# Residual loads moved ahead of the prefetch: two 512 KB loads of x issued one block earlier on ScalarE's queue

## The chip, the cores and the metric

The kernel runs as one program on the 8 cores of one Trainium2 chip. Each core computes one of the 8 batch entries, with no traffic between cores. The metric is device time in microseconds (us) of the slowest core.

## The reference, cut to what matters

```python
xn = _layernorm(x)                      # x: (8, 2048, 1024) f32, one batch entry per core
x = x + attn(xn) + ffn(xn)

def attn(x):                            # a linear recurrence over T=2048, written as a scan
    xn2 = layernorm(x) * ln_gamma + ln_beta
    y = scan(h = dA*h + dB*xn2;  y = C.h + D*xn2)
    return x + y @ W_out.T + b_out

def ffn(x):
    h = gelu(x @ ternary(W1).T + b1)    # 1024 -> 4096
    return h @ ternary(W2).T + b2       # 4096 -> 1024
```

The last step of the kernel computes, for each of 16 tiles of 128 rows, `h @ W2.T + y @ W_out.T` on TensorE and adds x (scaled and shifted by the row statistics of the first layernorm, which gives x + xn) and the biases on VectorE.

## The kernel before, in words

The program is a row of blocks. At the end of each block all engines meet in a barrier (the `UNCONDITIONAL_BRANCH` rows in the order of instructions). Every engine has its own list of instructions, written out by hand, with waits on semaphores between engines. DMAs are issued by SyncE (SP), by ScalarE (ACT) and by GpSimd (POOL) through the helper `sdma` (line 226), so every DMA issue shows line 226 in the profile. An instruction that ScalarE issues, be it a DMA or an activation, waits for all that stand ahead of it in ScalarE's list.

The stages: the statistics and normalization of x; a moment form of the recurrence, while the absolute sums of W1 and W2 are taken (activation L694, matmul L782); the first product of the feed-forward part (L1027), whose result goes through Gelu (L946) to tile `hst` and by SP to the scratch tensor `scr_h` in memory, while the ternary W2 is transposed into `W2T`. Then come the two blocks that the change touches.

The **W_out block** (lines 1084 to 1146). When `scr_h` is written, SP and ACT prefetch the hidden activations of the first two token groups (tg 0 and 1, 256 rows each) into the two buffers `hgrp`: SP loads the 16 even chunks of each group, ACT the 16 odd ones, so each issues 32 DMAs of 64 KB (128 rows of 512 bytes). POOL loads `bias1bc`, a row of 4 KB repeated to 128 partitions. Behind its 32 issues, in the same list, ACT converts the eight 128x1024 blocks of W_out to bf16 (`wob`, L1117); TensorE transposes each block (L1127) and VectorE copies it to `WoT` (L44 through a helper). The first two blocks of W_out are loaded earlier; POOL loads the other six into `wch`, each when ACT has converted the block two before it.

```python
for eb in range(8):
    swt(ac, f"w1c{eb % 2}", 16 * (eb // 2 + 1))
    if eb >= 2:
        ac.wait_ge(s_te, E_te_wo(eb - 2))
    bump(ac.activation(wob[eb % 2][:, :], wchunk[eb % 2][:, :], ...), "a2")
```

The **output block** (lines 1148 to 1237), 8 groups of 2 tiles (`tk` 0 and 1). TensorE makes 2 x (32 + 8) matmuls for a tile (L1186 with `hgrp` and `W2T`, L1193 with `yT` and `WoT`) into `ps_c` or `ps_e`. VectorE waits for the tile of x (`xr0` or `xr1`, 512 KB, 128 rows of 4 KB) and for TensorE, and makes four operations (line 44), and POOL stores the result. ACT only issues DMAs here. For the group tg it waits until TensorE is done with group tg-2 and issues 16 loads of `hgrp` (from tg 2 on), and then the two loads of `xr`, each (from tg 1 on) when VectorE is done with the tile of group tg-1 in the same buffer.

Of the kernel before, what the change touches and what calls it, by code (L numbers as in the profile page):

```python
# [98 lines left out]
def build_nc(debug_taps=False, stop_after=None):  # L99
    nc = bass.Bass("TRN2", target_bir_lowering=False)  # L100

    def din(name, shape, dtype=F32):
        return nc.dram_tensor(name, shape, dtype, kind="ExternalInput")

    x_in = din("x", [T, D])
# [40 lines left out]
    with st:  # L146
# [63 lines left out]
        def bump(inst, which, n=1):  # L210
            inst.then_inc(SEM[which], n)
            ctr[which] += n
            return ctr[which]
# [10 lines left out]
        def sdma(q, name, out, in_):  # L224
            s = streams[name]
            q.dma_start(out, in_).then_inc(s["sem"], 16)  # L226
            s["n"] += 16
            return s["n"]

        def swt(eng, name, val=None):  # L230
            s = streams[name]
            eng.wait_ge(s["sem"], s["n"] if val is None else val)  # L232
# [40 lines left out]
        with nc.Block() as blk:  # L273
            @blk.vector
            def _(dv):
                dv = _DR(dv)
                bump(dv.memset(xsq[:, :], 0.0), "dv")
# [793 lines left out]
        xr = [enD(nc.sbuf_tensor(f"xr{i}", [128, D], F32)) for i in range(2)]  # L1071
# [11 lines left out]
        with nc.Block() as blk:  # L1083
            @blk.gpsimd
            def _(gp):
                swt(gp, "srw", 16)
                swt(gp, "hw0", b5_hwv[0])
                swt(gp, "hw1", b5_hwv[1])
                sdma(gp, "cst", bias1bc[:, :], bass.AP(scr_rows, 0, [[0, 128], [1, D]]))
                for eb in range(2, 8):  # L1090
                    gp.wait_ge(s_a2, E_a2_wo(eb - 2))
                    sdma(gp, f"w1c{eb % 2}", wchunk[eb % 2][:, :],
                         Wout.ap()[eb * 128:(eb + 1) * 128, :])
            b6_cst = streams["cst"]["n"]

            @blk.sync
            def _(sy):
                swt(sy, "hw0", b5_hwv[0])
                swt(sy, "hw1", b5_hwv[1])
                for tg in range(2):  # L1100
                    for fc in range(0, 32, 2):
                        sdma(sy, f"hge{tg % 2}", hgrp[tg % 2][:, fc * 256:(fc + 1) * 256],
                             scr_h.ap()[fc, :, tg * 256:(tg + 1) * 256])

            @blk.scalar
            def _(ac):
                swt(ac, "hw0", b5_hwv[0])
                swt(ac, "hw1", b5_hwv[1])
                for tg in range(2):
                    for fc in range(1, 32, 2):  # L1110
                        sdma(ac, f"hgo{tg % 2}", hgrp[tg % 2][:, fc * 256:(fc + 1) * 256],
                             scr_h.ap()[fc, :, tg * 256:(tg + 1) * 256])
# [4 lines that stand above are left out]
                    bump(ac.activation(wob[eb % 2][:, :], wchunk[eb % 2][:, :],  # L1117
                                       AF.Copy, bias=0.0, scale=2.0), "a2")

            @blk.tensor  # L1120
            def _(te):
                for eb in range(8):
                    te.wait_ge(s_a2, E_a2_wo(eb))
                    if eb >= 1:
                        te.wait_ge(s_dv, E_dv_wo(eb - 1))
                    for dblk in range(8):
                        inst = te.transpose(ps_d[:, dblk * 128:(dblk + 1) * 128],  # L1127
                                            wob[eb % 2][:, dblk * 128:(dblk + 1) * 128],
                                            cID[:, :])
                    bump(inst, "te")  # L1130

            @blk.vector
            def _(dv):
                dv = _DR(dv)
                swt(dv, "hw0", b5_hwv[0])
                swt(dv, "hw1", b5_hwv[1])
                for eb in range(8):
                    dv.wait_ge(s_te, E_te_wo(eb))
                    bump(dv.tensor_copy(WoT3[:, :, eb * 128:(eb + 1) * 128], ps_d3), "dv")
# [8 lines left out]
        with nc.Block() as blk:  # L1148
# [8 lines left out]
            @blk.scalar  # L1157
            def _(ac):
                ac = _DR(ac)
                for tg in range(8):  # L1160
                    if tg >= 2:
                        ac.wait_ge(s_te, E_te_o(tg - 2, 1))
                        for fc in range(1, 32, 2):
                            sdma(ac, f"hgo{tg % 2}",
                                 hgrp[tg % 2][:, fc * 256:(fc + 1) * 256],
                                 scr_h.ap()[fc, :, tg * 256:(tg + 1) * 256])
                    for tk in range(2):
                        tci = tg * 2 + tk
                        if tg >= 1:
                            ac.wait_ge(s_dv, E_dv_oe(tg - 1, tk))  # L1170
                        sdma(ac, f"xr{tk}", xr[tk][:, :],
                             x_in.ap()[tci * 128:(tci + 1) * 128, :])

            @blk.tensor
            def _(te):
# [101 lines left out]
```

## Time and profile before

| what | us |
|---|---|
| two timed runs | 1138.73 and 1244.46, median 1191.6 |
| the profiled execution, its own time | 1137.69 |
| its span on the slowest core (core 7) | 1136.1 |
| spans of the eight cores | 1127.2 to 1136.1 |

The profile is that of core 7 in one execution. The span runs from the first to the last instruction on the core; 1.6 us of the execution's own time lie around it. In the picture of 40 slices each slice is 28.4 us long, a digit is the busy share in tenths. Times in the timeline are counted from the start of the span. "ACTq" and "SPq" are the queues' own instructions, here the issues of DMAs by ScalarE and SyncE.

### The profile page before, as it was taken

How to read it: one execution, taken by the hardware profiler on the slowest of the kernel's cores; microseconds unless marked ns; L12 is line 12 of the kernel's file. 1: busy time of each engine (PE TensorE's matmuls, PEld its weight loads, DVE VectorE, ACT ScalarE, POOL GpSimd, SP SyncE). 2: the span in 40 equal slices, each digit the busy share in tenths (PEclk: the TensorE clock that was granted, in tenths of full speed). 3: DMA queues.
4: the chain of work that ended last, by engine and by line, in shares of the span. 5: the costliest groups of instructions: out<-in, count | busy, mean ns of one | idle time of the engine just before them, and what ended most of it. 6: DMA issues, size and time to landing. Idle time of an engine off the chain costs nothing. (4 is left out here: it accounts for less than half of the span.)

```text
span 1136.1 us, 11816 instructions; the slowest of 8 cores (1127.2 to 1136.1 us)
## 1 busy us (share of the span) xinstructions
PE 755.1 (66%) x3622; PEld 321.7 (28%) x3622; DVE 430.1 (38%) x825; ACT 390.3 (34%) x481; POOL 109.2 (10%) x212
## 2 busy tenths in 40 slices
PE   0002222200899899819888888889049999999996
PEld 0000000100122122204444444444024444444442
DVE  3458888684354443422323232322011212212212
ACT  0033333200434344327888888887120000000000
POOL 1200000132111111100111111110010000000000
PEclk9999999999999999959999999999559999999998
DMA  4021111015555555523455545454641544345420
GB/s 72 1 70 55 57 57 53 14 25 98 174 173 166 154 178 178 176 62 142 168 179 184 175 171 181 168 179 155 169 164 38 135 126 127 80 127 148 113 73 38
DMA packets 78381, 136.41 MB, mean 120 GB/s; under 512 B 11448, under 2 KB 44656, under 8 KB 78320
## 3 DMA queue, kind: packets, MB, share of 16 engines
q0 software_dynamic: 22016, 67.64, 19.1%
q1 hardware_dynamic: 35568, 51.23, 14.5%
q10 hardware_dynamic: 20736, 16.79, 5.6%
q8 instruction: 31, 0.51, 0.2%
q14 instruction: 30, 0.25, 0.1%
HBM read 112.49 MB, written 25.19 MB: 121 GB/s over the span
## 5 line engine op out<-in xcount | busy, mean ns | idle before, releaser
L694 ACT ACTIVATE wabs<-wch 128x512 f32<-128x512 f32 x128 | 79.3, 628 | 122.7 <-DMA wch<-L_ffn_W 60.1
L1186 PE MATMUL ps_c<-W2T,hgrp 128*128 128x512 bf16 x512 | 115.7, 385 | 1.4 <-PEq L1083 1.4
L540 PE MATMUL ps_d<-sb_cID,xnb 128*128 128x128 bf16 x128 | 16.2, 306 | 149.5 <-ACT xnT L453 86.1
L1186 PE MATMUL ps_e<-W2T,hgrp 128*128 128x512 bf16 x512 | 113.1, 379 | 0.0
L795 PE MATMUL ps_c<-ub,sb_cP 128*128 128x512 bf16 x64 | 20.4, 450 | 82.4 <-DVE ub L717 82.4
L1186 PEld LDWEIGHTS ps_c<-W2T,hgrp 128*128 128x128 bf16 x512 | 50.7, 99 | 63.8 <-issue 5.0
L226 POOL DMA_DIRECT2D wch<-L_ffn_W x96 | 51.3, 535 | 175.8 <-ACT wabs L694 170.2
L1186 PEld LDWEIGHTS ps_e<-W2T,hgrp 128*128 128x128 bf16 x512 | 50.1, 98 | 60.4
L1027 PE MATMUL ps_a<-xnT,w1st 128*128 128x512 bf16 x256 | 62.2, 387 | 0.0
L712 DVE TENSOR_TENSOR ub<-xn2sb,mtb 128x512 bf16<-128x512 bf16 x128 | 45.7, 419 | 41.5 <-PE ps_c L799 23.2
L1027 PE MATMUL ps_b<-xnT,w1st 128*128 128x512 bf16 x256 | 60.6, 380 | 0.0
L1027 PE MATMUL ps_c<-xnT,w1st 128*128 128x512 bf16 x256 | 60.5, 379 | 0.0
L1027 PE MATMUL ps_e<-xnT,w1st 128*128 128x512 bf16 x256 | 60.5, 379 | 0.0
L782 PE MATMUL ps_a<-wabs,onesc 128*1 128x512 f32 x128 | 59.7, 610 | 0.0
L540 PEld LDWEIGHTS ps_d<-sb_cID,xnb 128*128 128x128 bf16 x128 | 12.4, 138 | 162.9 <-issue 162.9
L782 PE MATMUL ps_b<-wabs,onesc 128*1 128x512 f32 x128 | 58.0, 596 | 0.0
L990 DVE TENSOR_TENSOR w2tn<-wsgA,wsgB 128x1024 bf16<-128x1024 bf16 x32 | 22.1, 692 | 74.0 <-ACT wsgB L954 74.0
L44 DVE TENSOR_SCALAR t1f<-xr,stat_a,stat_b 128x1024 f32<-128x1024 f32 x8 | 6.5, 812 | 114.7 <-PE ps_c L1193 114.7
L984 DVE COPY w1st<-ps_d 128x1024 bf16<-128x1024 bf16 x30 | 20.7, 691 | 70.4 <-PE ps_d L1038 70.4
L44 DVE TENSOR_SCALAR t2f<-xr,stat_a,stat_b 128x1024 f32<-128x1024 f32 x8 | 6.5, 812 | 107.6 <-PE ps_e L1193 107.6
L934 ACT ACTIVATE wsgA<-wch,cst,invs 128x1024 bf16<-128x1024 f32 x30 | 37.2, 1240 | 29.0 <-DVE w2tn L990 27.9
L980 DVE TENSOR_TENSOR w1tn<-wsgA,wsgB 128x1024 bf16<-128x1024 bf16 x30 | 20.8, 693 | 61.0 <-ACT wsgB L937 61.0
(149 smaller groups left out, 1067.7 us busy)
## 6 DMA issues: line engine op xcount, KB each, us to landing
wch<-L_ffn_W SPq DMA_DIRECT2D x64, 256.0 KB, 3.5
wch<-L_ffn_W POOLq DMA_DIRECT2D x64, 256.0 KB, 3.9
wch<-L_ffn_W POOLq DMA_DIRECT2D x32, 512.0 KB, 5.4
wchC<-L_ffn_W POOLq DMA_DIRECT2D x32, 512.0 KB, 4.6
scr_h<-hst SPq DMA_DIRECT2D x32, 512.0 KB, 2.9
xt<-x SPq DMA_DIRECT2D x16, 512.0 KB, 3.3
hgrp<-scr_h SPq DMA_DIRECT2D x128, 64.0 KB, 4.1
hgrp<-scr_h ACTq DMA_DIRECT2D x128, 64.0 KB, 4.2
```

What stands on the lines that cost most here:

```text
L226: q.dma_start(out, in_).then_inc(s["sem"], 16)
L540: inst = te.transpose(ps_d[:, dblk * 128:(dblk + 1) * 128], xn_b[p][:, dblk * 128:(dblk + 1) * 128], cID[:, :])
L694: ac.activation(wabs[j % 4][:, :], wchunk[wk % 2][:, h * 512:(h + 1) * 512], AF.Abs).then_inc(s_wa, 1)
L712: dv._e.tensor_mul(u_b[k][:, hs], xn2sb[:, c * 1024 + h * 512: c * 1024 + (h + 1) * 512], mtb[:, k * D + h * 512: k * D + (h + 1) * 512])
L782: te.matmul(tgt[0:1, 0:512], onesc[:, 0:1], wabs[j % 4][:, :], start=(j % 16 == 0), stop=(j % 16 == 15)).then_inc(s_wm, 1)
L795: te.matmul(psy[:, sl], cP[:, k * 128:(k + 1) * 128], u_b[k][:, sl], start=(k == 0), stop=False)
L934: bump(ac.activation(wsgA[:, :], wchunk[k % 2][:, :], AF.Sign, bias=csl(C_NHALF), scale=invs[:, 0:1]), "a2")
L980: bump(dv.tensor_add(w1tn[:, :], wsgA[:, :], wsgB[:, :]), "dv")
L984: bump(dv.tensor_copy(w1st[k % 3].ap().rearrange("p (b f) -> p b f", f=128), ps_d3), "dv")
L990: bump(dv.tensor_add(w2tn[fc % 2][:, :], wsgA[:, :], wsgB[:, :]), "dv")
L1027: inst = te.matmul(psh, w1st[fc % 3][:, dblk * 128:(dblk + 1) * 128], xnT[:, dblk * T + t4 * 512: dblk * T + (t4 + 1) * 512], start=(dblk ...
L1186: te.matmul(pso[:, sl], hgrp[tg % 2][:, fc * 256 + tk * 128: fc * 256 + (tk + 1) * 128], W2T[:, fc * 1024 + dh * 512: fc * 1024 + (dh + 1) ...
```

## The change

The loads of `xr` for group 0 (both tiles) leave the output block, where they were ScalarE's first two instructions, and go to the W_out block, where they stand ahead of ScalarE's 32 loads of `hgrp`. In the output block the loads for the groups from 1 on stay where they were, with the same waits. Nothing else changes; the tiles `xr` are allocated before both blocks, and the semaphores count the same.

```diff
@@ -1106,6 +1106,9 @@
                 swt(ac, "hw0", b5_hwv[0])
                 swt(ac, "hw1", b5_hwv[1])
+                for tk in range(2):
+                    sdma(ac, f"xr{tk}", xr[tk][:, :],
+                         x_in.ap()[tk * 128:(tk + 1) * 128, :])
                 for tg in range(2):
                     for fc in range(1, 32, 2):
                         sdma(ac, f"hgo{tg % 2}", hgrp[tg % 2][:, fc * 256:(fc + 1) * 256],
@@ -1164,12 +1167,12 @@
-                    for tk in range(2):
-                        tci = tg * 2 + tk
-                        if tg >= 1:
+                    if tg >= 1:
+                        for tk in range(2):
+                            tci = tg * 2 + tk
                             ac.wait_ge(s_dv, E_dv_oe(tg - 1, tk))
-                        sdma(ac, f"xr{tk}", xr[tk][:, :],
-                             x_in.ap()[tci * 128:(tci + 1) * 128, :])
+                            sdma(ac, f"xr{tk}", xr[tk][:, :],
+                                 x_in.ap()[tci * 128:(tci + 1) * 128, :])
```

ScalarE's list in the W_out block and at the start of the output block, before and after (the line numbers of the kernel after are 3 higher from the first added line on):

```order
-L226 DMA hgrp<-scr_h 128x256 [waits st_hw0,st_hw1]
-L226 DMA hgrp<-scr_h 128x256 x31
-L1117 ACTIVATE wob<-wch 128x1024 [waits st_w1c0]
-L1117 ACTIVATE wob<-wch 128x1024 [waits st_w1c1]
...
+L226 DMA xr<-x 128x1024 [waits st_hw0,st_hw1]
+L226 DMA xr<-x 128x1024
+L226 DMA hgrp<-scr_h 128x256 x32
+L1120 ACTIVATE wob<-wch 128x1024 [waits st_w1c0]
+L1120 ACTIVATE wob<-wch 128x1024 [waits st_w1c1]
```

Two loads now stand between the barrier and the first load of `hgrp`, and every activation of the block stands behind 34 issues, where it stood behind 32. The second piece is again ScalarE's list, at the barrier between the W_out block and the output block:

```order
-L1157 UNCONDITIONAL_BRANCH [waits barrier_Pool_Activation_PE_DVE_SP_release]
-L226 DMA xr<-x 128x1024 x2
+L1160 UNCONDITIONAL_BRANCH [waits barrier_Pool_Activation_PE_DVE_SP_release]
 L226 DMA xr<-x 128x1024 [waits s_dv] x2
 L226 DMA hgrp<-scr_h 128x256 [waits s_te]
```

In the output block two loads without a wait are gone; the next rows are the same. The lists of the other four engines have the same instructions in the same places.

## Rows read from the trace of the kernel before

**Rows 1.** The page: the span in 40 slices of 28.4 us (busy tenths)
```profile
PE   0002222200899899819888888889049999999996
ACT  0033333200434344327888888887120000000000
DMA  4021111015555555523455545454641544345420
```

**Rows 2.** Timeline of core 7, the W_out block: start us, us, engine, line, what
```profile
801.56 20.45 SPq L226 DMA_DIRECT2D hgrp<-scr_h  x32
801.58 20.75 ACTq L226 DMA_DIRECT2D hgrp<-scr_h  x32
...
822.42 1.28 ACT L1117 ACT_TABLE_LOAD   x1 [24.65 <-issue]
823.71 2.00 ACT L1117 ACTIVATE wob<-wch 128x1024 bf16<-128x1024 f32 x2
...
825.33 0.53 POOL L226 DMA_DIRECT2D wch<-L_attn_W_out  x1 [22.72 <-ACT wob L1117]
...
829.79 1.06 ACT L1117 ACTIVATE wob<-wch 128x1024 bf16<-128x1024 f32 x1 [4.07 <-DMA wch<-L_attn_W_out]
...
845.58 0.69 DVE L44 COPY WoT<-ps_d 128x1024 bf16<-128x1024 bf16 x1 [1.98 <-PE ps_d L1127]
846.62 0.85 ACTq L226 DMA_DIRECT2D xr<-x  x2
...
846.91 9.63 PE L1186 MATMUL ps_c<-W2T,hgrp 128*128 128x512 bf16 x32 [1.44 <-PEq L1083]
...
858.11 7.07 PE L1186 MATMUL ps_c<-W2T,hgrp 128*128 128x512 bf16 x32
...
867.02 0.81 DVE L44 TENSOR_SCALAR t1f<-xr,stat_a,stat_b 128x1024 f32<-128x1024 f32 x1 [20.75 <-PE ps_c L1193]
```

**Rows 3.** Stretches of the output block: us, busy us (count) by engine, clock, DMA, GB/s
```profile
866.00:900.00 34.00, 34.00 (x160) 15.36 (x158) 7.08 (x8) 0.00 (x0) 1.07 (x2) 1.00 0.44 124
...
1060.00:1100.00 40.00, 40.00 (x187) 18.14 (x186) 7.83 (x9) 0.00 (x0) 1.59 (x3) 1.00 0.44 127
```

**Rows 4.** Instructions on tile xr: count, duration min/median/max ns; DMA to landing
```profile
L226 ACTq DMA_DIRECT2D xr<-x x16: 334/339/452, 846.6 to 1095.4; - x16
...
DMA to landing us min/median/max: 3.3/4.2/6.4
```

**Rows 5.** ScalarE's issues on tile hgrp: count, duration min/median/max ns
```profile
L226 ACTq DMA_DIRECT2D hgrp<-scr_h x128: 359/452/2659, 801.6 to 1070.8; - x128
```

**Rows 6.** Stretches of the prefetch: columns as in rows 3, the last three clock, DMA, GB/s
```profile
804.00:824.00 20.00, 0.00 (x0) 0.00 (x0) 0.00 (x0) 1.57 (x2) 0.00 (x0) 0.50 0.89 215
...
812.00:814.00 2.00, 0.00 (x0) 0.00 (x0) 0.00 (x0) 0.00 (x0) 0.00 (x0) 0.50 0.47 108
...
816.00:818.00 2.00, 0.00 (x0) 0.00 (x0) 0.00 (x0) 0.00 (x0) 0.00 (x0) 0.50 1.06 251
```

**Rows 7.** Stretches of the output block's first us, columns the same
```profile
848.00:849.00 1.00, 1.00 (x4) 0.30 (x2) 0.00 (x0) 0.00 (x0) 0.00 (x0) 0.50 0.91 352
849.00:850.00 1.00, 1.00 (x4) 0.45 (x3) 0.00 (x0) 0.00 (x0) 0.00 (x0) 0.50 1.03 406
...
852.00:853.00 1.00, 1.00 (x6) 0.50 (x5) 0.00 (x0) 0.00 (x0) 0.00 (x0) 0.93 0.00 0
```

**Rows 8.** DMA queues from 846 to 852 us: packets, MB, share of 16 engines
```profile
q10 hardware_dynamic: 287, 1.05, 46.5%
```

**Rows 9.** DMA queues from 801.5 to 810 us; q0 POOL's, q1 SP's, q10 ScalarE's
```profile
q0 software_dynamic: 144, 0.52, 25.9%
q1 hardware_dynamic: 708, 0.32, 17.0%
q10 hardware_dynamic: 637, 0.29, 12.6%
```

**Rows 10.** Timeline of core 0: its issues of the same block
```profile
795.88 17.63 ACTq L226 DMA_DIRECT2D hgrp<-scr_h  x32
```

## The prediction

> **What bounds the kernel now.** I read the picture of 40 slices first. TensorE is nearly full in the last 10 slices, and in the two before them it shows 0 and 4, while ScalarE shows 1 and 2 and the DMA engines 4 and 6 [rows 1]. That gap is the W_out block, the place where the change puts its two loads. Next the stretches of the output block: from 866 us on TensorE is busy 34.00 of 34.00 us and 40.00 of 40.00 us at the full granted clock [rows 3]. So once the output block runs, TensorE alone sets its end. ScalarE has only DMA issues there, and whatever delays the block's first matmul delays the end by as much.
>
> The timeline of the W_out block then shows what sets that first matmul [rows 2]. The barrier opens at about 801.5 us. ScalarE issues its 32 loads of `hgrp` for 20.75 us, up to 822.33. Only then come the table load (822.42) and the first two conversions of W_out (823.71). POOL's loads of further blocks of W_out wait for these (825.33, released by ScalarE's `wob`), ScalarE's third conversion waits for that load (829.79), and so on: load, convert, transpose, copy, until VectorE's last copy at 845.58. The barrier opens, and TensorE starts at 846.91. The two first conversions wait for nothing else: the idle time of 24.65 us ahead of the table load is given to "issue", and their data were there. So the path to the end is: 32 issues by ScalarE (20.75 us), the chain over W_out (822.33 to 846.91, 24.6 us), the output block. SyncE ends its issues at 822.01 as well, but no conversion waits for it.
>
> The 32 issues are not short because ScalarE is slow. One issue of `hgrp` takes 0.359 us at the least, 0.452 us in the median and 2.659 us at the most [rows 5]. At the median 32 would take 14.5 us; 20.75 us is 6.3 us more. During that stretch the DMA engines are busy 89% and move 215 GB/s, with single stretches at 1.06 and 251 GB/s [rows 6]. I read the long issues as ScalarE being held until its earlier transfers have moved. The Trainium skill ("DMA: Bandwidth & Descriptors", section "Issuing engines are not separate DMA queues") says that issuing from several engines saves only the sequencer's time and that this is usually small against the DMA itself; here the trace differs in what matters, since the issuing engine has work behind its issues and the 20.75 us of issuing are on the path.
>
> **The change, part by part.**
>
> *Removed: two issues at the start of the output block.* They take 0.85 us of ScalarE at 846.62 [rows 2], beside TensorE's matmuls, and nothing of ScalarE's is waited for there. Their data come 3.3 to 6.4 us after the issue [rows 4], so by 853.5 us at the latest. VectorE first reads them at 867.02, and there it is released by TensorE's `ps_c`, not by the load [rows 2]. The load had 13.5 us to spare. The gain is 0. Could it be more? The first 32 matmuls take 9.63 us where the next 32 take 7.07 [rows 2], and the loads of x move in just that time, so 2.56 us could be claimed for them. But until 852 the granted clock is 0.50 (1.2 GHz), and it was 0.50 all through the prefetch, in which TensorE had nothing to do [rows 6, 7]. The matmuls are slow by the clock, and nothing in the change makes TensorE busier before. I keep 0, with -2.56 us as the far bound.
>
> *Added: two issues ahead of the 32.* As bare instructions they cost 2 x 0.339 = 0.68 us on ScalarE [rows 4], and these are on the path, since every conversion stands behind them. This part no cover hides.
>
> *Added: 1.05 MB in a queue that is already held up.* By themselves the two loads took 46.5% of the 6 us from 846 to 852, that is 2.8 us of all 16 DMA engines [rows 8], at up to 406 GB/s [rows 7]. The prefetch has little free DMA time: 89% of 20 us leaves 2.2 us, much of it in single stretches such as that at 0.47 [rows 6]. From both sides: if the free time and the first 2.5 us, in which hardly anything moves, take in the loads, this costs 0; if they move at the mean rate of the prefetch, it is 1.05 MB / 215 GB/s = 4.9 us. I take 2.8 us, the engine time of the very same loads, as the nearest row. Here the loads of x would delay each later load of `hgrp` on ScalarE's queue, and by that its issue.
>
> *What stands behind.* The chain over W_out keeps its length. Its own loads start when the prefetch drains, before as after. The prefetched groups are not late: TensorE asks for group 0 only after the chain of 24.6 us. A later start of the output block moves all of it without changing it. ScalarE's further loads of `xr` wait for VectorE and TensorE as before. The allocation is the same and there is no new wait.
>
> The sum: 0 + 0.68 + 2.8 = +3.5 us. The profiled execution took 1137.69 us (its span 1136.1 and 1.6 us around it), so the forecast is 1137.7 + 3.5 = 1141.2 us. Of the two timed runs 1138.73 lies by this execution; the median of 1191.6 lies between it and 1244.46, which I do not use as a base.
>
> **The rivals.**
>
> *Hidden transfer (+0.7 us, 1138.4).* ScalarE's issues go on for 2.5 us before much data moves, and the DMA engines have 2.2 us free. If the loads of x fill these, only the two issues count. For it: core 0 issued its 32 in 17.63 us [rows 10], so not every core is held up as long as core 7. Against it: core 7 is the slowest core, and there 6.3 us of the issue time are already stalls.
>
> *SyncE gets ahead (+5.9 us, 1143.6).* Before, both queues run side by side and end together. While `bias1bc` with its 4 KB rows moved, it got 0.52 MB where the queues of `hgrp` got 0.32 and 0.29 [rows 9], 1.7 times one of them. If the loads of x share like this, SyncE's queue moves 1.05 / 1.7 = 0.62 MB meanwhile and is that far ahead, and ScalarE ends behind these bytes too: 0.62 MB / 251 GB/s = 2.4 us on top of the sum. For it: the queues share the same 16 engines. Against it: a queue that runs alone at the end is held up less, which gives part back. By the Trainium skill (same page, section "Queues, rings and completion order") each DMA engine takes turns between the queues packet by packet, which speaks for this rival; the rows show a share of 1.7 to 1 between large and small rows.
>
> *The slower side: a burst in which the memory collapses (+9.7 us or more, from 1147.4).* All eight cores now ask for their x at the same moment as for `scr_h`. If the loads moved at the rate of the poorest stretch, 108 GB/s [rows 6], they would cost 1.05 MB / 108 GB/s = 9.7 us. It becomes a slowdown by over 2% (22.8 us) only if the rate falls to 46 GB/s, or if ScalarE meets nine more stalls of the longest kind, 2.66 us [rows 5]. For it: issue times that differ between cores (17.63 and 20.75 us) and the poor stretch. Against it: 251 GB/s just after it, and 406 GB/s for these same loads when alone.
>
> *Faster after all (-5.4 us, 1132.3).* If large transfers at the head of ScalarE's queue made SyncE's queue wait and the rest of ScalarE's issues ran at their median, 34 issues would take 34 x 0.452 = 15.4 us, 5.4 us under 20.75. For it: core 0's 17.63 us lie on that side. Against it: there is more to move, and nothing takes work off. The 2.56 us of the slow matmuls, argued away above, would end on this side too.
>
> **How the numbers follow.** The forecast (stalls grow by about the loads' own DMA time) has a chance of 0.5, the hidden transfer 0.2, SyncE ahead 0.2, the collapse 0.06, the faster case 0.04. The first three lie between 1138.4 and 1143.6. Around each I put the difference that two executions show, as 1137.69 and 1138.73 here, and more where the slowest core may be another one (the cores' spans differ by 9 us). Down to the faster case's 1132.3 and up past the collapse's 1147.4 this gives a range of 1132.5 to 1151 us. A change by 2% is about what a measurement of this kernel can tell from none; that is 22.8 us either way, far outside of all sums. Faster by over 2%: 0.02, no case reaches it, only a disturbed comparison. Slower by over 2%: 0.04, the far end of the collapse. Within 2%: 0.94.
>
> **What would show it.** In the profile after: ScalarE's 34 issues from 801.5 us on should take about 24.3 us (20.75 + 3.5), by the hidden case 21.4, by SyncE's lead 26.6; SyncE should then end its 32 some 2 us or more before ScalarE. The table load to the first output matmul should again be 24.5 us, the 32 first matmuls again 9.6 us with the clock at 0.50, and VectorE's first operation on x again released by TensorE 20 us after the block's start. The reading is wrong if the issues take no longer than 20.75 us, if the time between table load and first matmul changes by over 2 us (then the loads of x disturb the loads of W_out), or if the first matmuls become faster. The prediction falls if the end moves by much more or less than the table load does.

## The result, and the profile after

| | us |
|---|---|
| before, median of 14 runs | 1136.76 |
| after, median of 15 runs | 1141.08 |
| ratio after to before | 1.0043, interval 1.0031 to 1.0056 |
| profiled execution after: its time, span of the slowest core (core 5) | 1144.99, 1143.5 |
| profiled execution before: the same (core 7) | 1137.69, 1136.1 |

The kernel became slower by 0.43%, that is 4.9 us (3.5 to 6.4) of 1136.76; the two medians of the table differ by 4.3 us, since the ratio is one of means. Runs in which one die of the chip ran at a lower clock are left out of the ratio; the 1244.46 us among the two times of before shown earlier was one of these.

The timeline of the slowest core after, in the W_out block. The rows answer to [rows 2]; the columns are the same.

```profile
805.03 22.49 SPq L226 DMA_DIRECT2D hgrp<-scr_h  x32
805.05 0.86 ACTq L226 DMA_DIRECT2D xr<-x  x2
805.56 0.53 POOL L226 DMA_DIRECT2D bias1bc<-scr_rows  x1 [18.53 <-POOLq L898]
805.94 23.02 ACTq L226 DMA_DIRECT2D hgrp<-scr_h  x32
829.04 1.28 ACT L1120 ACT_TABLE_LOAD   x1 [27.81 <-issue]
830.34 2.00 ACT L1120 ACTIVATE wob<-wch 128x1024 bf16<-128x1024 f32 x2
...
831.96 0.53 POOL L226 DMA_DIRECT2D wch<-L_attn_W_out  x1 [25.87 <-ACT wob L1120]
...
853.75 0.69 DVE L44 COPY WoT<-ps_d 128x1024 bf16<-128x1024 bf16 x1 [1.38 <-PE ps_d L1130]
...
855.08 8.87 PE L1189 MATMUL ps_c<-W2T,hgrp 128*128 128x512 bf16 x32 [1.44 <-PEq L1083]
...
874.42 0.81 DVE L44 TENSOR_SCALAR t1f<-xr,stat_a,stat_b 128x1024 f32<-128x1024 f32 x1 [19.98 <-PE ps_c L1196]
```

ScalarE issues from 805.05 to 828.96: 23.9 us, where it was 20.75 in [rows 2]. From the table load to the first output matmul it is 26.0 us (24.5 before on core 7), and VectorE's first operation on x is released by TensorE as before, so the early load gives nothing back. The block, from SyncE's first issue to the first output matmul, takes 50.05 us on this core and took 45.35 on core 7: 4.7 of the 7.4 us between the two spans. Another 3.5 us is where the block starts, 805.03 against 801.56, in stages that the change does not touch, and the output block is 0.8 us shorter. So the difference between these two single profiles (7.4 us) overstates the change; the ratio comes from many runs (4.9 us).

Since single cores scatter, the table below gives the mean over the eight cores of each profile, each number a difference between the starts of rows like those above: issue time is from SyncE's first issue to ScalarE's table load, chain from there to the first output matmul, rest from there to the end of the span.

| us, mean of 8 cores | issue time | chain | block | rest |
|---|---|---|---|---|
| before | 19.1 | 24.2 | 43.2 | 288.7 |
| after | 22.3 | 24.7 | 46.9 | 288.3 |
| difference | +3.2 | +0.5 | +3.7 | -0.4 |

What the change adds lies in the block, and there mostly in ScalarE's issues (3.2 of 3.7 us). The spans themselves grew by 5.6 us in the mean; the other 2.3 us are a later start of the block (798.8 us before, 801.1 after), in stages that the change does not touch. The block's length ranges from 41.6 to 45.4 us over the cores before, and from 43.9 to 50.1 after.

Where do the bytes go? The DMA queues of core 5 after, in the first 8 us of the block (packets, MB, share of the 16 engines; q10 is ScalarE's, q1 SyncE's, q0 POOL's), and the DMA share and rate in the stretch of the prefetch, which answers to [rows 6]:

```profile
q10 hardware_dynamic: 342, 1.08, 40.7%
q0 software_dynamic: 83, 0.34, 22.4%
q1 hardware_dynamic: 359, 0.17, 10.3%
```

```profile
805.00:824.00 19.00, 0.00 (x0) 0.00 (x0) 0.00 (x0) 0.00 (x0) 0.53 (x1) 0.50 0.87 207
824.00:829.00 5.00, 0.00 (x0) 0.00 (x0) 0.00 (x0) 0.00 (x0) 0.00 (x0) 0.50 1.01 251
```

In the first 8 us ScalarE's queue moves almost nothing but the loads of x, and SyncE's loads of `hgrp` get 0.17 MB through, where they got 0.32 MB in the first 8.5 us before [rows 9]. The engines are busy 87% up to 824 us and 101% from there to the end of the issues (a share of 1.01 means full), so the bytes that are still to move find no free room.

### The profile page after: what moved, and what is told of

It reads as the page before. It is cut to its first block and busy times, and to the rows that moved or that the text cites. A ratio compares the mean times of both kernels' runs of the same rounds, so it can differ in the third digit from the quotient of the medians.

```text
span 1143.5 us, 11816 instructions; the slowest of 8 cores (1129.9 to 1143.5 us)
## 1 busy us (share of the span) xinstructions
PE 756.9 (66%) x3622; PEld 321.3 (28%) x3622; DVE 430.3 (38%) x825; ACT 390.4 (34%) x481; POOL 109.2 (10%) x212
## 5 line engine op out<-in xcount | busy, mean ns | idle before, releaser
L795 PE MATMUL ps_c<-ub,sb_cP 128*128 128x512 bf16 x64 | 19.8, 439 | 81.8 <-DVE ub L717 81.8
L1189 PEld LDWEIGHTS ps_e<-W2T,hgrp 128*128 128x128 bf16 x512 | 50.1, 98 | 60.4
L782 PE MATMUL ps_b<-wabs,onesc 128*1 128x512 f32 x128 | 61.0, 616 | 1.8 <-ACT wabs L694 1.7
L712 DVE TENSOR_TENSOR ub<-xn2sb,mtb 128x512 bf16<-128x512 bf16 x128 | 45.7, 422 | 43.2 <-PE ps_c L799 25.5
L990 DVE TENSOR_TENSOR w2tn<-wsgA,wsgB 128x1024 bf16<-128x1024 bf16 x32 | 22.1, 692 | 74.0 <-ACT wsgB L954 74.0
L984 DVE COPY w1st<-ps_d 128x1024 bf16<-128x1024 bf16 x30 | 20.7, 691 | 69.2 <-PE ps_d L1038 69.2
L980 DVE TENSOR_TENSOR w1tn<-wsgA,wsgB 128x1024 bf16<-128x1024 bf16 x30 | 20.8, 693 | 61.9 <-ACT wsgB L937 61.9
```

What stands on the lines that cost most here:

```text
L712: dv._e.tensor_mul(u_b[k][:, hs], xn2sb[:, c * 1024 + h * 512: c * 1024 + (h + 1) * 512], mtb[:, k * D + h * 512: k * D + (h + 1) * 512])
L782: te.matmul(tgt[0:1, 0:512], onesc[:, 0:1], wabs[j % 4][:, :], start=(j % 16 == 0), stop=(j % 16 == 15)).then_inc(s_wm, 1)
L980: bump(dv.tensor_add(w1tn[:, :], wsgA[:, :], wsgB[:, :]), "dv")
L984: bump(dv.tensor_copy(w1st[k % 3].ap().rearrange("p (b f) -> p b f", f=128), ps_d3), "dv")
L990: bump(dv.tensor_add(w2tn[fc % 2][:, :], wsgA[:, :], wsgB[:, :]), "dv")
L1189: te.matmul(pso[:, sl], hgrp[tg % 2][:, fc * 256 + tk * 128: fc * 256 + (tk + 1) * 128], W2T[:, fc * 1024 + dh * 512: fc * 1024 + (dh + 1) ...
```

## The experiments

My theory: two loads ahead of the conversions in ScalarE's list lengthen the path by their issues and by the DMA time of their bytes, because ScalarE is held until its queue has room. Rivals: the cost is the issues alone, or the number of rows; only the queue in which they stand matters; or moving the bytes out of the output block costs by itself. All ratios are to the kernel before, with their 95% intervals; the times in the text are means over eight cores, as in the table above. In the edits, `...` and words in brackets stand for lines that are left out.

The experiments ran on three other occasions, each beside runs of the kernel before: e1, e2, e4 and e5 on one chip, e3, e6, e7 and e8 on a second, e9 and e10 on a third. There the kernel before took 1138.9 to 1140.0 us in the mean, against 1136.6 us beside the kernel after, and it was not profiled again. So the ratios compare like with like, but where a block or an issue time of an experiment is set against the tables above, 2 us or so may lie between the occasions. The kernel after was not run again either: differences between it and an experiment have that uncertainty too.

**e1_behind_conv: the loads behind the conversions, in the same block.** Against the kernel after:

```diff
-                for tk in range(2):
-                    sdma(ac, f"xr{tk}", xr[tk][:, :], ...)
                 for tg in range(2):
                     (32 loads of hgrp)
                 for eb in range(8):
                     (conversions)
+                for tk in range(2):
+                    sdma(ac, f"xr{tk}", xr[tk][:, :], ...)
```

> The two loads of xr stay in the W_out block but stand behind ScalarE's eight conversions. Theory (what counts is that they stand ahead of the conversions in ScalarE's list): the mean over the cores of ScalarE's issue time goes back to 19 us (22.3 in the kernel after), the end is that of the kernel before, ratio 0.998 to 1.001. Rival (moving 1.05 MB out of the output block into the busy block costs by itself): ratio 1.003 or more.

Measured: 0.9997 (0.998 to 1.0014), issue time 18.8 us, chain 25.4 us, rest 288.7 us. On the slowest core the two loads are now issued at 842.69, 3.7 us ahead of the first output matmul. With nothing of ScalarE's and no other load of the block behind them they cost nothing that the runs can tell. It is the position ahead of the prefetch and the conversions that costs, and taking the loads out of the output block has no benefit either.

**e3_tiny: the issues without the bytes.** Against the kernel before, ahead of the 32 loads:

```diff
+                for tk in range(2):
+                    sdma(ac, f"xr{tk}", xr[tk][:, 0:16],
+                         x_in.ap()[tk * 128:(tk + 1) * 128, 0:16])
```

The full loads stay in the output block, behind a wait for these.

> The kernel before, with two extra loads of xr cut to 16 of 1024 columns (64 bytes a row, 128 rows, the same number of rows as in the full loads) ahead of ScalarE's 32 loads; the full loads stay in the output block. Theory (of the 3.2 us, 0.7 to 0.9 are the two issues and the rest the bytes): ScalarE's issue time 19.7 to 20.2 us in the mean of the cores, ratio 1.000 to 1.002. Rival (the number of rows or issues in the queue counts, not the bytes): 22.3 us as in the kernel after, ratio 1.003 or more.

Measured: 1.0002 (0.9989 to 1.0016), issue time 20.2 us. Two issues with 128 rows each cost 1.1 us of issue time in this profile and nothing that the timed runs can tell; the rival, 1.003 or more, is out. The rest of the 3.2 us, and nearly all of the slowdown, is the bytes.

**e5_double: twice the bytes.** Against the kernel after, behind its two loads (VectorE also waits for the extra data before its first use of the buffers):

```diff
+                for tk in range(2):
+                    sdma(ac, "tap", osb[tk][:, :],
+                         x_in.ap()[(2 + tk) * 128:(3 + tk) * 128, :])
```

> Four loads of 512 KB stand ahead of ScalarE's 32 loads: the two of the kernel after and two more of x into the output buffers, whose data nobody uses. Theory (each 1.05 MB ahead costs some 3.2 us of issue time on the path): ScalarE's issue time 25 to 26 us in the mean of the cores, ratio to before 1.006 to 1.009. Rival (a fixed cost of the first large load, or free room): as the kernel after, 22.3 us, 1.004. Rival (SyncE gets ahead more and more): 28 us or more, 1.009 and over.

Measured: 1.0067 (1.0041 to 1.0094), issue time 26.9 us, chain 24.5 us. The slowest core's timeline:

```profile
806.54 26.28 SPq L226 DMA_DIRECT2D hgrp<-scr_h  x32
806.55 0.87 ACTq L226 DMA_DIRECT2D xr<-x  x2
807.06 0.53 POOL L226 DMA_DIRECT2D bias1bc<-scr_rows  x1 [18.53 <-POOLq L898]
807.45 1.49 ACTq L226 DMA_DIRECT2D osb<-x  x2
808.97 26.03 ACTq L226 DMA_DIRECT2D hgrp<-scr_h  x32
835.09 1.28 ACT L1123 ACT_TABLE_LOAD   x1 [32.35 <-issue]
```

The issue time grows by 7.8 us over before, for four loads, where two gave 3.2: somewhat more than in proportion (I had expected 25 to 26 us). The ratio, 7.6 us, is as expected and gives 3.8 us for each pair of loads. SyncE, which has no new loads, takes 24.7 us in the mean where it took 18.6 before and 20.7 after. So the bytes hold up both queues, ScalarE's more.

**e2_on_sp: the same loads at the head of SyncE's queue.** Against the kernel after:

```diff
@@ sync
+                for tk in range(2):
+                    sdma(sy, f"xr{tk}", xr[tk][:, :], ...)
                 for tg in range(2):
                     (SyncE's 32 loads of hgrp)
@@ scalar: the loads of xr removed
```

> The two loads of xr are issued by SyncE, ahead of its 32 loads of hgrp; ScalarE's list in the W_out block is that of before. Theory A (the bytes delay whoever shares the 16 DMA engines): ScalarE's issue time is some 2 to 3 us over before, SyncE's more, ratio 1.002 to 1.003. Theory B (only the queue in which the loads stand is held up): ScalarE's issue time 19 us as before, SyncE's 22, ratio 1.000.

Measured: 1.0023 (1.0008 to 1.0037), ScalarE's issue time 21.4 us, SyncE's 22.1. ScalarE's list is that of before and it still takes longer: theory A. The slowest core of this kernel:

```profile
804.34 0.81 SPq L226 DMA_DIRECT2D xr<-x  x2
804.36 23.39 ACTq L226 DMA_DIRECT2D hgrp<-scr_h  x32
...
827.83 1.28 ACT L1120 ACT_TABLE_LOAD   x1 [27.28 <-issue]
```

With no issue added to ScalarE, its 32 loads take 23.39 us here. So at least a part of the slowdown is sharing the 16 DMA engines, whoever issues. How large a part is open: the ratios (0.0023 of 0.0043) say half, but their intervals overlap, and by the profiles it is more, with a block of 46.4 us against 46.9 after and 43.2 before. This agrees with the Trainium skill ("DMA: Bandwidth & Descriptors", section "Issuing engines are not separate DMA queues"), by which DMAs of all issuing engines run on the same 16 engines and interleave.

**e4_after_issues: the loads between the 32 issues and the conversions.** Against the kernel after:

```diff
-                for tk in range(2): (loads of xr)
                 for tg in range(2): (32 loads of hgrp)
+                for tk in range(2): (loads of xr)
                 for eb in range(8): (conversions)
```

> The two loads of xr stand between ScalarE's 32 loads of hgrp and its conversions. If the 3.2 us more of issue time come from the loads' bytes ahead of the later issues, they shrink here to the two issues and the wait of these for room, 0.7 to 1.5 us, but the loads of W_out now meet 1.05 MB more: the chain from the table load to the first output matmul grows from 24.2 to 25 to 27 us, ratio 1.001 to 1.004. If only the number of issues ahead of the conversions counts, the issue time is 22.3 us as in the kernel after and the chain is unchanged.

Measured: 1.0021 (1.0001 to 1.0041), issue time 19.8 us, chain 27.7 us, a little over the 25 to 27 expected. The cost has moved: now the first further block of W_out waits behind the loads of x.

```profile
822.83 0.93 ACTq L226 DMA_DIRECT2D xr<-x  x2
823.85 1.28 ACT L1120 ACT_TABLE_LOAD   x1 [25.21 <-issue]
...
826.76 0.53 POOL L226 DMA_DIRECT2D wch<-L_attn_W_out  x1 [23.28 <-ACT wob L1120]
...
833.95 1.06 ACT L1120 ACTIVATE wob<-wch 128x1024 bf16<-128x1024 f32 x1 [6.81 <-DMA wch<-L_attn_W_out]
```

ScalarE waits 6.81 us for the load of W_out, 4.07 before [rows 2]. In the profiles the 1.05 MB cost 3.2 to 4.2 us of block in all three places ahead of loads on which the block depends (e2, after, e4); the ratios of e2 and e4 say 2.4 to 2.6 us.

The next kernels ask the reverse: if what stands ahead of the conversions is on the path, taking it away must gain.

**e6_two_conv_first: the first two conversions ahead of the issues.** Against the kernel before:

```diff
+                for eb in range(2): (conversions)
                 for tg in range(2): (32 loads of hgrp)
-                for eb in range(8): (conversions)
+                for eb in range(2, 8): (conversions)
```

> The kernel before, but ScalarE's first two conversions of W_out, whose data are there, stand ahead of its 32 loads. If the path is ScalarE's list and then the chain over W_out, the table load and two conversions (3.3 us) now come first, but the loads of W_out blocks 2 and 3 run beside the issues and the 4.1 us of wait for them behind the issues go away, and with them the 3.3 us of conversions behind the issues: end of the block 3 to 6 us earlier than before, ratio 0.995 to 0.998. If the DMA engines alone set the end of the block, no gain.

Measured: 0.9969 (0.9958 to 0.998), 3.5 us, as expected. The block, 41.6 us in the mean, is only 1.6 us shorter than in the profile of before, where I expected 3 to 6; the rest may be the difference between the occasions.

**e7_issues_off_act: ScalarE starts with the conversions.** SyncE issues all of group 0 and the even loads of group 1, ScalarE the odd ones of group 1 behind its conversions.

```diff
@@ sync
-    for tg in range(2): for fc in range(0, 32, 2): sdma(sy, ...)
+    for fc in range(32):       (group 0, even and odd)
+    for fc in range(0, 32, 2): (group 1, even)
@@ scalar
-    (16 odd loads of group 0 and of group 1)
     for eb in range(8): (conversions)
+    for fc in range(1, 32, 2): (group 1, odd)
```

> The kernel before, with ScalarE's list in the W_out block turned round: SyncE issues all 32 loads of group 0 and the 16 even ones of group 1, ScalarE starts with the conversions and issues its 16 loads of group 1 behind them. Theory (the 20 us of issues on the path are there only by ScalarE's order): block 43.2 us falls to 26 to 31 us, the chain being some us longer as its loads meet the prefetch; ratio 0.985 to 0.990. Rival (the bytes moved set the block's end, whoever issues them): 36 us or more, ratio over 0.993.

Measured: 0.995 (0.9929 to 0.9971), block 39.3 us: a miss, by my own theory, and what the rival (the bytes) forecast. The slowest core shows two reasons, the first of which is the rival's:

```profile
801.82 27.75 SPq L226 DMA_DIRECT2D hgrp<-scr_h  x48
801.89 1.28 ACT L1116 ACT_TABLE_LOAD   x1 [3.87 <-PEq L898]
...
812.52 1.06 ACT L1116 ACTIVATE wob<-wch 128x1024 bf16<-128x1024 f32 x1 [7.33 <-DMA wch<-L_attn_W_out]
...
833.67 7.59 ACTq L226 DMA_DIRECT2D hgrp<-scr_h  x16
836.08 0.69 DVE L44 COPY WoT<-ps_d 128x1024 bf16<-128x1024 bf16 x1 [3.42 <-PE ps_d L1129]
842.36 3.19 PE L1188 MATMUL ps_c<-W2T,hgrp 128*128 128x512 bf16 x7 [6.39 <-PEq L1083]
```

Beside the prefetch the waits for the W_out loads are longer (7.33 us the first, 4.07 in [rows 2]; 23.2 against 12.2 us in sum), so the last copy starts only 34.3 us after the block's start. And the barrier does not open at the last copy (836.08) but when ScalarE has issued its 16 loads (841.26), though nobody needs group 1 yet: TensorE waits 6.39 us at it.

**e8_wout_ahead: in addition, W_out into six free buffers at once.** (ScalarE converts each block from its new buffer when its load has landed.)

```diff
+    wt8 = [wchunk[0], wchunk[1], osb[0], osb[1], t1f, t2f, xr[0], xr[1]]
     for eb in range(2, 8):
-        gp.wait_ge(s_a2, E_a2_wo(eb - 2))
-        sdma(gp, f"w1c{eb % 2}", wchunk[eb % 2][:, :], Wout...)
+        sdma(gp, f"wo{eb}", wt8[eb][:, :], Wout...)
```

> As the kernel with the issues off ScalarE, and in addition the six later blocks of W_out are loaded at once into six buffers that are free in this block (the output, temporary and xr tiles), ahead of the load of the biases. Theory: the chain then goes at the pace of transpose and copy, 2 to 2.7 us a block, once the data are there: block 18 to 25 us, ratio 0.978 to 0.984. If the transfers (3.1 MB of W_out, 2.1 MB of group 0) set it at 215 to 250 GB/s, block 25 to 28 us, ratio 0.984 to 0.988.

Measured: 0.9906 (0.9885 to 0.9927), block 33.8 us, again short of what I expected, and the chain is not the reason:

```profile
809.15 34.61 SPq L227 DMA_DIRECT2D hgrp<-scr_h  x48
...
829.76 0.69 DVE L44 COPY WoT<-ps_d 128x1024 bf16<-128x1024 bf16 x1 [1.26 <-PE ps_d L1133]
844.13 0.85 ACTq L227 DMA_DIRECT2D xr<-x  x2
...
844.42 1.01 PE L1192 MATMUL ps_c<-W2T,hgrp 128*128 128x512 bf16 x2 [14.77 <-PEq L1084]
```

The last copy of W_out starts at 829.76, 20.6 us after the block's start. TensorE waits 14.77 us at the barrier (14.2 to 15.7 on all cores), which opens only once SyncE's last issue ends at 843.76. But the barrier alone does not explain this wait: by the trace the last load of group 0 lands at 841.81, 2.6 us ahead of the first matmul (1.5 to 3.3 on all cores), so without the barrier TensorE would have waited for its data for all but these. In e7, in contrast, group 0 had landed 14.4 to 18.8 us ahead of the first matmul, and there the 5.8 to 6.4 us at the barrier (1.44 before) are the barrier's own. Loads of group 1, needed some 36 us after the output block's start (an estimate: an eighth of its 288.7 us), stand ahead of a barrier, and ScalarE's 16 of them, issued from 827.02 on, share the DMA engines with the rest of group 0. The next two kernels take group 1 away.

**e9_group1_later: the kernel before, with group 1 loaded in the output block.**

```diff
@@ W_out block, sync and scalar
-                for tg in range(2):
+                for tg in range(1):
@@ output block, sync
-                for tg in range(2, 8):
-                    sy.wait_ge(s_te, E_te_o(tg - 2, 1))
+                for tg in range(1, 8):
+                    if tg >= 2:
+                        sy.wait_ge(s_te, E_te_o(tg - 2, 1))
@@ output block, scalar, behind the loads of xr for group 0
+                    if tg == 0:
+                        for fc in range(1, 32, 2): sdma(ac, "hgo1", ...)
```

> The kernel before, with the 32 loads of group 1 (16 by ScalarE, 16 by SyncE) moved from the W_out block to the start of the output block, where they are needed 35 us later. Theory (ScalarE's issues ahead of the conversions are on the path, one for one, with the DMA time of what stands with them): ScalarE's issue time falls from 19 us to 8 to 10 us, the chain stays at 24 to 26 us, block 33 to 35 us, ratio 0.990 to 0.993. Rival (the loads then hold up the first matmuls of group 1, or the loads of x, and give it back): ratio 0.996 or more.

Measured: 0.9899 (0.9862 to 0.9937), issue time 9.3 us, chain 25.2 us, block 34.5 us, rest 288.5 us. Half of the issues take half of the time, the block is 8.7 us shorter, and the output block takes nothing back. The ratio is at the good end of what was expected (0.990 to 0.993). This is the mirror of the change: what is needed late is issued late.

**e10_both: e8 with group 1 in the output block.** The edits of the two together.

> The kernel with W_out loaded ahead and SyncE issuing the 32 loads of group 0, in which TensorE waited 14.8 us at the barrier for engines that were still issuing loads of group 1; here the loads of group 1 stand in the output block as in the previous kernel. Theory: the barrier comes when the last conversion or SyncE's 32nd issue is done, 21 to 26 us after the block's start (43.2 before), ratio 0.981 to 0.986. Rival (the bytes of W_out and group 0 set it): 28 us or more, ratio over 0.987.

Measured: 0.9834 (0.9802 to 0.9867), median 1121.82 us, the ratio as expected and the block, 26.7 us, just over the 21 to 26. The slowest core:

```profile
801.76 35.98 SPq L227 DMA_DIRECT2D hgrp<-scr_h  x48
...
822.24 0.69 DVE L44 COPY WoT<-ps_d 128x1024 bf16<-128x1024 bf16 x1 [1.31 <-PE ps_d L1127]
827.22 0.87 ACTq L227 DMA_DIRECT2D xr<-x  x2
828.11 11.06 ACTq L227 DMA_DIRECT2D hgrp<-scr_h  x16
830.85 9.21 PE L1192 MATMUL ps_c<-W2T,hgrp 128*128 128x512 bf16 x32 [8.71 <-DMA hgrp<-scr_h]
```

(The profile merges SyncE's 32 issues of group 0 with its 16 of group 1.) On all eight cores TensorE is now released by the data of group 0, and no longer by the barrier. Group 0 lands 26.5 us after the block's start, 31.5 in e8 (means), so of the 7.1 us between the two blocks 5 are earlier data and 2 are the barrier. The barrier still comes late, though: ScalarE is past it at 827.22, some 4 us after the last copy, and the data come 3.6 us after that. It is the fastest version, 1.7% under the kernel before; what ends its block is the transfer of group 0.

## Why the prediction was right or wrong, point by point

**What bounds the kernel.** Right. The path is ScalarE's issues, the chain over W_out, the output block; e1, e6 and e9 move only what stands ahead of the conversions, and the time follows in direction. In size it fell by 1.3 to 2.8 us more than the block from e6 to e10 (3.5 against 1.6 us in e6, 11.5 against 8.7 in e9), about as much as lies between the occasions.

**Removed, gain 0.** Right within what the runs tell: e1, with the loads out of the output block and nothing ahead of the conversions, is at 0.9997. The first 32 matmuls take 8.87 us on core 5 after, where no DMA moves beside them from 855 to 856 us and the granted clock is 0.50, and took between 8.80 and 9.89 us on the cores before; the next 32 take 7.07 in both kernels. So the 2.56 us were not the loads' doing.

**Added: two issues, 0.68 us.** The size fits what can be told: e3 shows 1.1 us in one profile and 0.2 us (-1.3 to 1.8) in the timed ratio.

**Added: 1.05 MB, 2.8 us.** The mechanism was right: the issues lengthen by the bytes ahead of them (e3 and e5). That ScalarE is held for want of room in its queue is my reading of this; no run shows the queue itself. In the mean of the cores the size was right as well: the issue time grew by 3.2 us for a forecast of 3.5, the block by 3.7, on the slowest core the issues took 23.9 us where 24.3 were forecast. By the timed ratios it may be too small: 4.9 us less e3's 0.2 leave an estimate of 4.7 us for the bytes, close to the prediction's upper bound of 4.9, while e5's 7.6 us for two pairs of loads give 3.8 us for bytes and issues together. That the true price is above 2.8 us is not clear of the noise, since the interval of the change starts at 3.5 us.

**The rival that SyncE gets ahead** was partly true and I kept it out of the sum. SyncE ended its issues 0.3 us ahead of ScalarE before and 1.5 us ahead after, in the mean of the cores, where the rival wanted 2 or more, and in e2 ScalarE's issue time is 21.4 instead of 22.3 us with the loads in the other queue. By these two differences it adds an estimated 1 us, where its own sum had 2.4; that is no more than single profiles scatter. The hidden transfer, the collapse and the faster case did not come: 22.3 us of issue time against 19.8, 28.8 and 15.4 (19.1 plus 0.7, 19.1 plus 9.7, 34 issues at the median).

**What stands behind.** Right in the sum (the chain 24.2 and 24.7 us, the rest 288.7 and 288.3).

**The step that failed is the one from the sum to the verdict.** The sum said slower by 3.5 us, with the forecast and its two likeliest rivals all above zero. The verdict then took 2% (22.8 us) as "about what a measurement of this kernel can tell from none" and gave 0.94 to "within 2%", so it named no direction. No run stood behind the 2%: the only number near it was the difference of 1137.69 and 1138.73, 0.1%. The runs showed a comparison that tells 0.13% either way, and in it a clear slowdown, 1.0043 (1.0031 to 1.0056). The base makes it worse: beside the median of 1191.6 us of two runs the forecast of 1141.2 us reads as a gain of 4%. The prediction was right to set that median aside (the median of 14 runs is 1136.76), but its verdict did not say "slower" against the base that it used.

The forecast time was met more closely than the change: 1141.2 us against 1141.08, but from a base of 1137.7 instead of 1136.76. The change itself is 4.9 us (3.5 to 6.4), with the forecast of 3.5 at the lower end. If the sum is too small, the term is the 2.8 us for the bytes, for which the estimate above is 3.8 us with the issues (e5) to 4.7 us without them. Another way to lose more than the mean's 3.7 us would be that the slowest of eight cores loses more than the others: the sum was made on core 7 of one profile, and the blocks spread over 3.8 us before and 6.2 us after. Over the timed runs the slowest core's span lies 5.4 us above the mean of the eight in the kernel after and 4.4 to 4.7 us in the kernel before on the three other occasions, but also 5.1 us in e1, which costs nothing. So this stays open.

## What to carry to other kernels

A load that is moved earlier "because the queue is free there" must be looked up in the list of the engine that issues it: in this kernel everything behind it, compute included, waited for its issue and, the DMA engines being busy, for its bytes. And a forecast is held against what repeated runs can tell (0.13% here), not against a round figure. Order prefetches by when their data are needed, keep those that are needed late behind the barrier and behind the compute of the issuing engine, and load first what the next chain depends on. Here the change brought forward 1.05 MB that had 13.5 us to spare and paid 4.9 us; the opposite move, putting the 2.1 MB of group 1 later, gained 1%, and 1.7% together with W_out loaded at once and ScalarE's issues handed to SyncE.

## What the runs showed of the hardware that I had not expected

- An issue of a load cost its engine far more than its shortest time (0.36 us) while the DMA engines were full: 32 loads of 64 KB took 17.3 to 20.8 us on the cores before, for a median issue of 0.45 us, and 26.0 us on the slowest core in e5. The 16 loads of group 0 alone took 9.3 us (e9).
- Loads with long rows at the head of one queue held up the other queue also: in 8 us ScalarE's queue moved 1.08 MB in 342 packets and SyncE's 0.17 MB in 359 packets. In packets these two got about the same, in bytes they did not; POOL's queue got 83 packets in that time. For the two this fits the Trainium skill ("DMA: Bandwidth & Descriptors", section "Queues, rings and completion order"), by which a DMA engine takes turns between queues at the granularity of packets; whether a packet of the profile is one in the page's sense, no run here shows.
- The barrier waited for engines that only issued DMAs: 5.8 to 6.4 us of TensorE's time in e7 (1.44 before), with its inputs landed; of the 14.77 us in e8 only the last 2.6.
